# Expert rows of a mixture-of-experts layer: row fetches on two alternating semaphores, each issued ahead of the same turn's scatter

## The chip, the cores and the metric

One core of one Trainium2 chip. The metric is device time in microseconds (us) of one launch. Engines are named as the profile names them: PE is TensorE (PEld its weight loads), DVE is VectorE, ACT is ScalarE, POOL is GpSimd, SP is SyncE. Each has a sequencer of its own (a "q" behind the name, as in POOLq) that takes waits, branches and issues.

## What is computed

A graph layer on 12,500 nodes of 256 features, then a top-2 mixture of 64 experts, a batch normalisation and a residual layer normalisation. The change touches the experts alone:

```python
x = gc + (feats @ W_res + b_res)                 # per node, 256 wide
vals, idx = top_k(x @ Wg + bg, 2)                # two experts for each node
gates = softmax(vals)
# for every (node, expert) pair, by expert:
h1 = gelu(x[tok] @ w1[e] + b1[e])                # 256 -> 512
h2 = h1 @ w2[e] + b2[e]                          # 512 -> 256
core[tok] += gate * h2
```

## The kernel before

The program runs in stages: edges are sorted and counted, messages are gathered and summed (to about 2400 us), then `experts` (L1460) runs, then `norms`. In `experts` the pairs of one expert are cut into **turns** of 128 rows. The kernel works out at run time how many turns there are. 232 scatters were issued in the profiled execution, four of them after the last turn that has matmuls.

One turn g passes through the engines like this:

- **POOL** fetches the 128 rows of x of a turn with an indirect DMA (`fetch`, L1563 to L1566) into one of four places of `ring`, and later writes the turn's result rows out with another indirect DMA, a scatter into `picked` (`send`, L1568 to L1575). Row numbers are in `rows_at`, target rows in `places`.
- **ACT** copies the fetched rows to `xs` (`take`, L1537 to L1543) and applies the four gelus of the turn (L1548), in the order gelus of g, then `take(g + 2)`. After the last turn of an expert it also issues three DMAs that load the weights of an expert three ahead (`load_weights`, L275 to L277). The weights have four places.
- **PE** does sixteen matmuls with w1 (L1681), turns the next rows (two transposes, L1674), and does eight matmuls with w2 (L1688).
- **DVE** copies the turned rows (`xst`, L1621), adds b2 (`ysum`, L1648) and, in `scale` (L1625 to L1640), sets the next row numbers, the target rows and the gate, and multiplies into one of the **two** result buffers `ys[:, 0]` and `ys[:, 1]`.

What sets the order on POOL is the loop `quad` (L1586 to L1595), four turns a round. Step n of it is: wait until scatter n-1 has landed (`y_sent`, L1590), tell DVE that this buffer is free (`freed`, L1591), wait for DVE's result n (`y_set`, L1570), issue scatter n (L1573), wait until the fetches of all rows up to n+3 have landed (`rows_in`, L1593), issue the fetch of row block n+4. DVE's `scale(n)` waits for `freed` n+1 before it writes `places` (L1633), so scatter n-2 has landed by then. ACT's `take(g)` waits for `rows_in` itself. All fetches count up one semaphore, one after the other, and so never two are in flight.

Of the kernel before, what the change touches and what calls it, by code (L numbers as in the profile page):

```python
# [41 lines left out]
def gnn_layer(nc, x, src, dst, W_gc, b_gc, W_res, b_res, Wg, bg, w1, b1, w2, b2, gamma, beta, out):  # L42
# [35 lines left out]
    with ExitStack() as ctx:  # L78
# [178 lines left out]
        with ExitStack() as stage:  # L257
            def tmp(name, shape, dt):
                return stage.enter_context(nc.sbuf_tensor(name, shape, dt))

            HOT_W = 4 * (PER + 1) // 2 * P
            W1, W2 = HELD * KD * H, HELD * KH * D
            work = tmp("work", [P, (RING + 1) * (D + 1) + HOT_W], F32)
            assert W1 + W2 + HELD * D <= (RING + 1) * (D + 1)
            w1s = work[:, 0:W1].rearrange("p (u k h) -> p u k h", u=HELD, k=KD)
            w2s = work[:, W1:W1 + W2].rearrange("p (u k d) -> p u k d", u=HELD, k=KH)
            b2s = work[:, W1 + W2:W1 + W2 + HELD * D].rearrange("p (u d) -> p u d", u=HELD)
            table = tmp("table", [P, 4, (X + HELD) * (CAP // P)], F32)
            base_of = tmp("base_of", [1, X + 1 + HELD], I32)
            b1_cols = tmp("b1_cols", [P, KH, X], F32)  # L270
            w_in = [ctx.enter_context(nc.semaphore(f"w_in{u}")) for u in range(HELD)]

            def load_weights(eng, e, u):

                eng.dma_start(w1s[:, u, :, :], w1[bass.ds(e, 1), :, :].rearrange("a (k p) h -> p (a k) h", p=P)).then_inc(w_in[u], 16)  # L275
                eng.dma_start(w2s[:, u, :, :], w2[bass.ds(e, 1), :, :].rearrange("a (k p) d -> p (a k) d", p=P)).then_inc(w_in[u], 16)
                eng.dma_start(b2s[:, u, :], b2[bass.ds(e, 1), :].broadcast_to([P, D])).then_inc(w_in[u], 16)  # L277

            with nc.cleanup_on_exit():
                aggregate(nc, x, W_res, b_gc, b_res, W_gc, Wg, bg, b1, h_table, x1_rows, m_base, base_out, zeros_out, acc3, work, ident, ones,  # L280
                          iota_f, place_lo, src_cols, rel_cols, where, valid, table, base_of, b1_cols, load_weights, ps,
                          N=N, D=D, X=X, H=H, KD=KD, KH=KH, AW=AW, CH=CH, PER=PER, EARLY=EARLY, LATE=LATE, NT=NT, LAST=LAST)
            experts(nc, x1_rows, picked, w1s, w2s, b2s, w_in, load_weights, ident, table, base_of, b1_cols, ps, D=D, X=X, H=H, KD=KD, KH=KH,
                    ROW=ROW, PLACES=N * TOP_K)
# [1175 lines left out]
def experts(nc, x1_rows, picked, w1s, w2s, b2s, w_in, load_weights, ident, table, base_of, b1_cols, ps, D, X, H, KD, KH, ROW, PLACES):  # L1460

    with ExitStack() as part:
        def t2(name, shape, dt):
            return part.enter_context(nc.sbuf_tensor(name, shape, dt))

        def sem2(name):
            return nc.alloc_semaphore(name)

        U = HELD
        R = 4  # L1470
# [3 lines left out]
        rows_at = t2("rows_at", [P, R], I32)  # L1474
# [8 lines left out]
        ys = t2("ys", [P, 2, D], F32)  # L1483
        warm = t2("warm", [P, 1], F32)

        rows_in = sem2("ring_in")
        first_rows_at = sem2("first_rows_at")
        order_set = sem2("order_set")
        xs_set = sem2("xs_set")
# [8 lines left out]
        y_set = sem2("y_set")  # L1498
        y_sent = [sem2("y_sent0"), sem2("y_sent1")]
        freed = sem2("ys_freed")  # L1500
        carrier = sem2("x_carrier")

        def bounds(engine, e, more=0):

            _, g = nc.values_load_multi_w_load_instructions(
                base_of[0:1, bass.ds(e, U + 1 + more)], engines=[engine], min_val=0, max_val=X * CAP // SUP,
                skip_runtime_bounds_check_because="sums of the experts' turns, 1 to CAP // SUP each")
            return g

        def turns_in_all(engine):  # L1510
            return nc.values_load(base_of[0:1, X:X + 1], engines=[engine], min_val=X, max_val=X * CAP // SUP,
                                  skip_runtime_bounds_check_because="the sum of the experts' turns")

        def each_expert(eng, engine, before, turn, follow=None, more=0):


            def some(i, followed):
                starts = bounds(engine, U * i, more)
                for u in range(U):
                    e = U * i + u  # L1520
                    before(e, i, u, starts)
                    with eng.Fori(starts[u], starts[u + 1]) as g:
                        turn(e, u, g, starts[u])
                    if u < followed:
                        follow(e + U - 1, (u - 1) % U, starts[u])
            if follow is None:
                with eng.Fori(0, X // U) as i:
                    some(i, 0)
            else:
                with eng.Fori(0, X // U - 1) as i:  # L1530
                    some(i, U)
                some(X // U - 1, 1)

        with nc.Block() as block:
            @block.scalar
            def _(act):
                def take(g):  # L1537

                    act.wait_ge(rows_in, 16 * (g + 1))

                    if not isinstance(g, int) or g > 0:
                        act.wait_ge(xs_turned, g)
                    nc.scalar.copy(xs[:, :], ring[:, g % R, 0:D]).then_inc(xs_set, 1)  # L1543

                def turn(e, u, g, g0):
                    for h in range(KH):
                        act.wait_ge(h_done, g * KH + h + 1)
                        nc.scalar.activation(hid[:, h, :], ps[:, h, 0:SUP], ACT.Gelu,  # L1548
                                             bias=b1_cols[:, h, bass.ds(e, 1)]).then_inc(h_set, 1)
                    take(g + 2)  # L1550

                def follow(e, u, g0):

                    act.wait_ge(ysum_set, g0 + 1)
                    load_weights(act, e, u)

                nc.scalar.activation(warm[:, :], b1_cols[:, 0, 0:1], ACT.Gelu)
                take(0)
                take(1)
                each_expert(act, EngineType.Activation, lambda *a: None, turn, follow)  # L1560

            @block.gpsimd
            def _(pool):  # L1563
                def fetch(u):
                    pool.indirect_dma_start(out=ring[:, u, :], out_offset=None, in_=x1_rows[:, :],  # L1565
                                            in_offset=bass.IndirectOffsetOnAxis(ap=rows_at[:, u:u + 1], axis=0)).then_inc(rows_in, 16)  # L1566

                def send(n, u):  # L1568
                    b = u % 2
                    pool.wait_ge(y_set, n + 2)  # L1570
                    pool.sem_inc(carrier, 1)

                    pool.indirect_dma_start(out=picked[:, :], out_offset=bass.IndirectOffsetOnAxis(ap=places[:, b:b + 1], axis=0),  # L1573
                                            in_=ys[:, b, :], in_offset=None, bounds_check=PLACES - 1,
                                            oob_is_err=False).then_inc(y_sent[b], 16)  # L1575

                pool.wait_ge(first_rows_at, 1)
                for u in range(R):
                    if u > 0:
                        pool.wait_ge(rows_in, 16 * u)  # L1580
                    fetch(u)
                pool.sem_inc(freed, 1)

                quads = (turns_in_all(EngineType.Pool) + R) // R

                def quad(j):  # L1586
                    for u in range(R):
                        n = R * j + u
                        if not isinstance(n, int) or n > 0:
                            pool.wait_ge(y_sent[1 - u % 2], 32 * j + 16 * ((u + 1) // 2))  # L1590
                        pool.sem_inc(freed, 1)  # L1591
                        send(n, u)
                        pool.wait_ge(rows_in, 16 * (n + R))  # L1593
                        pool.sem_inc(carrier, 1)
                        fetch(u)  # L1595
                quad(0)
                with pool.Fori(1, quads) as j:
                    quad(j)
                pool.wait_ge(y_sent[0], 32 * quads)
                pool.sem_inc(carrier, 1)  # L1600
                pool.wait_ge(y_sent[1], 32 * quads)
                pool.sem_inc(carrier, 1)
                pool.wait_ge(rows_in, 64 * quads + 64)
                pool.sem_inc(carrier, 1)

            @block.vector
            def _(dve):
# [363 lines left out]
```

## Time and profile before

| what | us |
|---|---|
| median of 3 runs | 3764.92 (3763.87 to 3767.51) |
| the profiled execution | 3769.93 |
| its span in the profile | 3768.2 |
| first to last scatter of `experts` | 1019.3 (2429.6 to 3448.9) |
| PE busy in that stretch | 892.32, granted clock 0.99 |
| POOL busy in that stretch | 459.66 |
| one fetch, one scatter on POOL | 0.978, 1.011 |

A span is what the profiler saw between first and last instruction; 1.7 us lie around it. Busy time on POOL is the time in which it writes out a DMA's descriptors, not the transfer. The profiled execution is 5.0 us above the median. "Granted clock" is the share of TensorE's full clock that the chip let through, 1.00 for 2.4 GHz and 0.50 for 1.2 GHz.

### The profile page before, as it was taken

The numbers are of one execution on the slowest core, as the hardware profiler recorded it, in microseconds if no ns is written. First come the engines' busy times: TensorE is split into PE (matmuls) and PEld (weight loads), VectorE is DVE, ScalarE is ACT, GpSimd is POOL, SyncE is SP. The second block draws the span as 40 slices with busy tenths as digits, with TensorE's granted clock in tenths as the row PEclk, the third lists the DMA queues.
The fourth block names the chain that finished last, engine by engine and source line by source line (L and its number), as shares of the span: only waits on it lengthen the run. The fifth ranks groups of instructions, "written<-read, shape, count | busy, mean of one in ns | idle before, by whom it ended". The sixth has DMA issues, their size and how long they took to land. (4 is left out here: it accounts for less than half of the span.)

```text
span 3768.2 us, 61533 instructions
## 1 busy us (share of the span) xinstructions
PE 3028.5 (80%) x16520; PEld 2198.4 (58%) x16684; DVE 1867.6 (50%) x6028; ACT 1083.0 (29%) x2679; POOL 2136.5 (57%) x2194
## 2 busy tenths in 40 slices
PE   3747889898899888898998898789888898894710
PEld 3523555555555555555555555588777887884610
DVE  6982444444444444444444444544443444443878
ACT  3950222222222222222222222233333333331123
POOL 3006777777777777777777777244444444442122
PEclk9878999999999999999999999899999999997865
DMA  8635444444444444444444444334344343434634
GB/s 351 223 102 159 126 118 128 128 118 128 128 117 128 118 128 128 117 129 127 118 128 121 125 117 118 112 120 133 120 134 147 118 131 124 136 121 135 204 107 145
DMA packets 287579, 509.98 MB, mean 135 GB/s; under 512 B 43417, under 2 KB 201200, under 8 KB 284738
## 3 DMA queue, kind: packets, MB, share of 16 engines
q0 software_dynamic: 102192, 274.64, 25.7%
q10 hardware_dynamic: 73042, 123.41, 9.4%
q1 hardware_dynamic: 112192, 109.95, 9.1%
q8 instruction: 89, 1.46, 0.2%
q14 instruction: 64, 0.52, 0.0%
HBM read 404.99 MB, written 107.63 MB: 136 GB/s over the span
## 5 line engine op out<-in xcount | busy, mean ns | idle before, releaser
L1150 POOL DMA_INDIRECT work<-h_table,src_cols x1661 | 1575.5, 949 | 728.0 <-issue 426.2
L1436 PE MATMUL ps<-work 128*128 128x257 f32 x3322 | 1063.2, 402 | 208.5 <-DMA work<-h_table,src_cols 185.2
L1436 PEld LDWEIGHTS ps<-work 128*128 128x128 f32 x3322 | 563.8, 192 | 556.5 <-issue 301.5
L1342 PE MATMUL ps<-none_w,none 128*128 128x512 bf16 x2213 | 677.1, 383 | 5.5 <-issue 0.4
L1565 POOL DMA_INDIRECT ring<-x_rows,rows_at x236 | 230.8, 978 | 484.8 <-DMA ring<-x_rows,rows_at 235.5
L1688 PE MATMUL ps<-work,hid 128*128 128x256 f32 x1824 | 445.0, 387 | 72.5 <-ACT hid L1548 70.5
L1681 PEld LDWEIGHTS ps<-xst,work 128*128 128x128 f32 x3648 | 444.9, 193 | 25.6 <-issue 13.4
L1681 PE MATMUL ps<-xst,work 128*128 128x128 f32 x3648 | 448.6, 276 | 8.2 <-issue 7.4
L1185 DVE TENSOR_TENSOR acc<-acc,ps 128x257 f32<-128x257 f32 x98 | 41.5, 423 | 780.6 <-PE ps L1333 780.6
L1688 PEld LDWEIGHTS ps<-work,hid 128*128 128x128 f32 x1824 | 328.7, 190 | 134.3 <-ACT hid L1548 97.9
L1342 PEld LDWEIGHTS ps<-none_w,none 128*128 128x128 bf16 x2344 | 224.7, 99 | 160.1 <-issue 3.8
L1548 ACT ACTIVATE hid<-ps,b_cols 128x128 f32<-128x128 f32 x912 | 269.2, 368 | 142.8 <-PE ps L1681 99.2
L1573 POOL DMA_INDIRECT picked<-ys,places x232 | 234.6, 1011 | 127.6 <-issue 100.9
L1648 DVE TENSOR_TENSOR ysum<-ps,work 128x256 f32<-128x256 f32 x228 | 96.9, 425 | 397.9 <-PE ps L1688 397.9
L1170 DVE TENSOR_TENSOR work<-rel_cols,ps 128x1152 f32<-128x1152 f32 x196 | 250.6, 1280 | 64.2 <-PE ps L1436 63.4
L1543 ACT COPY xs<-ring 128x256 f32 (+1 forms) x230 | 93.1, 405 | 509.6 <-DMA ring<-x_rows,rows_at 509.6
L1116 ACT COPY acc<-ps 128x256 f32<-128x256 f32 x98 | 36.6, 373 | 651.0 <-PE ps L1375 651.0
L1122 ACT COPY turned<-ps 128x512 f32<-128x512 f32 x98 | 57.4, 586 | 473.3 <-PE ps L1362 473.3
L733 ACT ACTIVATE stairs<-iota_f,lo_half 128x128 bf16<-128x128 f32 x624 | 183.0, 388 | 32.9 <-DVE lo_half L675 32.0
L1795 POOL TENSOR_TENSOR pk<-pk,beta_b 128x1792 f32<-128x1792 f32 x14 | 64.1, 4585 | 225.2 <-DMA pk<-in_x_dram 225.2
L1205 DVE TENSOR_TENSOR logits<-ps,gate_bias 128x64 f32<-128x64 f32 x98 | 22.0, 225 | 281.3 <-PE ps L1389 281.3
L1621 DVE COPY xst<-ps 128x256 f32<-128x256 f32 x229 | 97.3, 425 | 121.9 <-PE ps L1674 112.4
(256 smaller groups left out, 3806.4 us busy)
## 6 DMA issues: line engine op xcount, KB each, us to landing
work<-in_L_gnn_w_dram ACTq DMA_DIRECT2D x122, 512.0 KB, 4.6
work<-h_table,src_cols POOLq DMA_INDIRECT x1661, 2.8
picked<-acc ACTq DMA_DIRECT2D x1, 25088.0 KB, 102.1
pk<-picked SPq DMA_DIRECT2D x28, 896.0 KB, 8.1
m_base<-acc ACTq DMA_DIRECT2D x1, 12642.0 KB, 37.0
acc<-m_base SPq DMA_DIRECT2D x14, 903.0 KB, 6.5
x_rows<-acc SPq DMA_DIRECT2D x98, 129.0 KB, 2.4
xr_x<-in_x_dram SPq DMA_DIRECT2D x97, 128.0 KB, 2.3
```

Source lines behind the costliest of these rows:

```text
L733: mm = nc.scalar.activation(stairs[:, k, n, :], iota_f[:, :], ACT.Sign, scale=-1.0, bias=lo_half[:, bass.ds(g * PIECES + 2 * WHOLE + n, 1)])
L1150: pool.indirect_dma_start(out=got[:, c % RING, 0:D], out_offset=None, in_=h_table[:, :], in_offset=bass.IndirectOffsetOnAxis(ap=src_cols[: ...
L1170: nc.vector.tensor_tensor(hot[:, (2 * t + h) % HOTS, 0:b - a, :], rel_cols[:, a:b].unsqueeze(2).broadcast_to([P, b - a, P]), lanes.unsquee ...
L1342: nc.tensor.matmul(ps[:, 7, :], none[:, :], none_w[:, :], start=False, stop=False)
L1436: nc.tensor.matmul(ps_flat[:, bank(t, k, w[0])], hot[:, (2 * t + (k >= HALF)) % HOTS, k % HALF if k >= HALF else k, :], got[:, c % RING, : ...
L1548: nc.scalar.activation(hid[:, h, :], ps[:, h, 0:SUP], ACT.Gelu, bias=b1_cols[:, h, bass.ds(e, 1)]).then_inc(h_set, 1)
L1565: pool.indirect_dma_start(out=ring[:, u, :], out_offset=None, in_=x1_rows[:, :], in_offset=bass.IndirectOffsetOnAxis(ap=rows_at[:, u:u + 1 ...
L1573: pool.indirect_dma_start(out=picked[:, :], out_offset=bass.IndirectOffsetOnAxis(ap=places[:, b:b + 1], axis=0), in_=ys[:, b, :], in_offse ...
L1621: nc.vector.tensor_copy(xst[:, :, :], ps[:, 6, 0:KD * SUP].rearrange("p (k n) -> p k n", k=KD)).then_inc(xst_set, 1)
L1648: nc.vector.tensor_tensor(ysum[:, :], ps[:, 4, 0:D], b2s[:, u, :], ALU.add).then_inc(ysum_set, 1)
L1681: mm = nc.tensor.matmul(ps[:, h, 0:SUP], w1s[:, u, k, h * P:(h + 1) * P], xst[:, k, :], start=(k == 0), stop=(k == KD - 1))
L1688: mm = nc.tensor.matmul(ps[:, 4, 0:D], hid[:, h, :], w2s[:, u, h, :], start=(h == 0), stop=(h == KH - 1))
```

## The change

The fetches use two semaphores by turns (even and odd row blocks), so that two fetches may be in flight. ACT no longer waits for a fetch itself but for `rows_ready`, which POOL counts up once it has seen a fetch land. In a step, POOL now waits for row block n+2 (instead of n+3), counts up `rows_ready`, waits for scatter n-1 and for result n as before, and then issues the fetch of block n+4 and behind it scatter n. The result buffers stay two.

```diff
-        rows_in = sem2("ring_in")
+        rows_in = [sem2("ring_in0"), sem2("ring_in1")]
+        rows_ready = sem2("rows_ready")
...
                 def take(g):
-                    act.wait_ge(rows_in, 16 * (g + 1))
+                    act.wait_ge(rows_ready, g + 1)
...
-                                            in_offset=bass.IndirectOffsetOnAxis(ap=rows_at[:, u:u + 1], axis=0)).then_inc(rows_in, 16)
+                                            in_offset=bass.IndirectOffsetOnAxis(ap=rows_at[:, u:u + 1], axis=0)).then_inc(rows_in[u % 2], 16)
...
                 def send(n, u):
                     b = u % 2
-                    pool.wait_ge(y_set, n + 2)
-                    pool.sem_inc(carrier, 1)
...
-                for u in range(R):
-                    if u > 0:
-                        pool.wait_ge(rows_in, 16 * u)
-                    fetch(u)
+                fetch(0)
+                fetch(1)
+                for u in range(2):
+                    pool.wait_ge(rows_in[u], 16)
+                    pool.sem_inc(rows_ready, 1)
+                    fetch(u + 2)
...
                         n = R * j + u
+                        pool.wait_ge(rows_in[u % 2], 32 * j + 16 * (u // 2 + 2))
+                        pool.sem_inc(rows_ready, 1)
                         if not isinstance(n, int) or n > 0:
                             pool.wait_ge(y_sent[1 - u % 2], 32 * j + 16 * ((u + 1) // 2))
                         pool.sem_inc(freed, 1)
-                        send(n, u)
-                        pool.wait_ge(rows_in, 16 * (n + R))
+                        pool.wait_ge(y_set, n + 2)
                         pool.sem_inc(carrier, 1)
                         fetch(u)
+                        send(n, u)
```

On POOL, in the first two steps of the loop (before the counted rounds begin). The list names semaphores by the number's first owner: before, `x_in_any` is the fetches' `rows_in`, `any_gathered3` is `y_set`, `any_gathered4` and `any_gathered5` are `y_sent` 0 and 1. Before:

```order
L1573 DMA picked<-ys,places 25088x256 [waits any_gathered3]
L1565 DMA ring<-x_rows,rows_at 128x258 [waits x_in_any]
L1573 DMA picked<-ys,places 25088x256 [waits any_gathered4,any_gathered3]
L1565 DMA ring<-x_rows,rows_at 128x258 [waits x_in_any]
L1573 DMA picked<-ys,places 25088x256 [waits any_gathered5,any_gathered3]
```

After the change `x_in_any` and `scaled_any` are the two semaphores of the fetches, `any_gathered5` is `y_set`, `any_gathered6` and `any_gathered7` are `y_sent` 0 and 1:

```order
L1565 DMA ring<-x_rows,rows_at 128x258 [waits x_in_any,any_gathered5]
L1570 DMA picked<-ys,places 25088x256
L1565 DMA ring<-x_rows,rows_at 128x258 [waits scaled_any,any_gathered6,any_gathered5]
L1570 DMA picked<-ys,places 25088x256
L1565 DMA ring<-x_rows,rows_at 128x258 [waits x_in_any,any_gathered7,any_gathered5]
```

All waits of a step now stand ahead of its fetch, the one for the scatter before (`y_sent`) among them, and the scatter comes last, with no wait of its own.

## Rows read from the trace of the kernel before

**Rows 1.** Whole page: its head and costliest groups (count, busy, mean ns, idle before).

```profile
span 3768.2 us, 61533 instructions
...
L1565 POOL DMA_INDIRECT ring<-x_rows,rows_at x236 | 230.8, 978 | 484.8 <-DMA ring<-x_rows,rows_at 235.5
...
L1573 POOL DMA_INDIRECT picked<-ys,places x232 | 234.6, 1011 | 127.6 <-issue 100.9
```

**Rows 2.** Windows from first to last scatter: busy (count) by engine, clock, DMA share.

```profile
2429.60:3448.90 1019.30, 892.32 (x5881) 802.69 (x5879) 430.81 (x1671) 357.13 (x1130) 459.66 (x462) 0.99 0.40 126
```

**Rows 3.** Waits, 2650 to 3450 us: total us, times, longest.

```profile
ACT xs L1543 <- DMA ring<-x_rows,rows_at: 403.1, 177, 4.5
...
POOL ring L1565 <- DMA ring<-x_rows,rows_at: 182.1, 120, 4.1
POOL ring L1565 <- DMA picked<-ys,places: 148.0, 47, 4.3
```

**Rows 4.** Timeline, 3006 to 3020 us: start, duration, engine, line, idle before and releaser.

```profile
3006.84 0.98 POOL L1565 DMA_INDIRECT ring<-x_rows,rows_at  x1 [1.99 <-DVE ys L1639]
3008.13 1.01 POOL L1573 DMA_INDIRECT picked<-ys,places  x1 [0.30 <-issue]
...
3008.97 1.95 PE L1681 MATMUL ps<-xst,work 128*128 128x128 f32 x16
...
3010.41 0.98 POOL L1565 DMA_INDIRECT ring<-x_rows,rows_at  x1 [1.27 <-DMA ring<-x_rows,rows_at]
...
3012.70 1.95 PE L1681 MATMUL ps<-xst,work 128*128 128x128 f32 x16
...
3013.40 0.41 ACT L1543 COPY xs<-ring 128x256 f32 x1 [1.97 <-DMA ring<-x_rows,rows_at]
...
3013.75 0.38 ACTq L275 DMA_DIRECT2D work<-in_L_gnn_w_dram  x1
...
3013.95 0.98 POOL L1565 DMA_INDIRECT ring<-x_rows,rows_at  x1 [1.21 <-DMA ring<-x_rows,rows_at]
...
3019.93 0.98 POOL L1565 DMA_INDIRECT ring<-x_rows,rows_at  x1 [3.45 <-DMA picked<-ys,places]
```

**Rows 5.** All instructions of line L275 (weight loads) issued by ACT.

```profile
L275 ACTq DMA_DIRECT2D work<-in_L_gnn_w_dram x61: 383/385/434, 2434.3 to 3393.5; - x61
```

**Rows 6.** Timeline, 3403 to 3411 us, POOL.

```profile
3403.70 1.01 POOL L1573 DMA_INDIRECT picked<-ys,places  x1 [2.89 <-issue]
...
3407.22 1.10 POOL L1573 DMA_INDIRECT picked<-ys,places  x1 [1.23 <-issue]
...
3410.77 1.01 POOL L1573 DMA_INDIRECT picked<-ys,places  x1 [1.16 <-DMA picked<-ys,places]
```

**Rows 7.** Timeline, 3433 to 3440 us, behind the last matmuls.

```profile
3433.84 0.98 POOL L1565 DMA_INDIRECT ring<-x_rows,rows_at  x1 [2.41 <-DMA ring<-x_rows,rows_at]
3434.23 0.15 DVE L1633 CAST places<-in_order  x1 [2.39 <-POOLq L1591]
...
3435.13 1.01 POOL L1573 DMA_INDIRECT picked<-ys,places  x1 [0.30 <-issue]
...
3439.85 1.01 POOL L1573 DMA_INDIRECT picked<-ys,places  x1 [0.30 <-DVE ys L1639]
```

**Rows 8.** Timeline, 2433 to 2438 us: scatters around a weight load.

```profile
2433.53 1.00 POOL L1573 DMA_INDIRECT picked<-ys,places  x1 [1.65 <-issue]
...
2434.30 0.43 ACTq L275 DMA_DIRECT2D work<-in_L_gnn_w_dram  x1
...
2437.04 1.00 POOL L1573 DMA_INDIRECT picked<-ys,places  x1 [1.23 <-issue]
```

**Rows 9.** Timeline, 3161 to 3169 us: a scatter right behind a weight load.

```profile
3161.57 0.38 ACTq L275 DMA_DIRECT2D work<-in_L_gnn_w_dram  x1
...
3162.27 1.02 POOL L1573 DMA_INDIRECT picked<-ys,places  x1 [3.12 <-issue]
...
3168.16 0.15 DVE L1633 CAST places<-in_order  x1 [1.57 <-POOLq L1591]
```

**Rows 10.** Timeline (two rows) and windows (the third) around 2460 us.

```profile
2461.46 2.40 PE L1688 MATMUL ps<-work,hid 128*128 128x256 f32 x8 [2.93 <-ACT hid L1548]
...
2463.66 3.22 PE L1681 MATMUL ps<-xst,work 128*128 128x128 f32 x16
...
2463.00:2466.00 3.00, 3.00 (x14) 2.83 (x13) 1.41 (x6) 1.07 (x3) 0.98 (x1) 0.50 0.04 12
```

More of the change, by code:

```diff
@@ L1602, in _ @@
                 pool.sem_inc(carrier, 1)
-                pool.wait_ge(rows_in, 64 * quads + 64)
-                pool.sem_inc(carrier, 1)
+                for u in range(2):
+                    pool.wait_ge(rows_in[u], 32 * quads + 32)
+                    pool.sem_inc(carrier, 1)
             @block.vector
```

## Prediction

> **What bounds the kernel now.** I read the page first, then the windows, the waits and the timeline of `experts`. The reader should see on the page that POOL issues 236 fetches and 232 scatters of about 1 us each [rows 1]. In the windows, the stretch from first to last scatter is 1019.3 us, so a turn costs 1019.3 / 232 = 4.39 us; PE is busy for 892.32 of it, and its clock is full [rows 2]. In the waits, ACT waits 177 times for a fetch, 403.1 us in 800, and POOL waits again and again for a landing before its next fetch [rows 3].
>
> The timeline says why. Two chains run nearly at the same pace. Undisturbed, PE starts a turn's w1 matmuls 3.73 us after the last turn's (3008.97 to 3012.70), and the fetches, one at a time, start 3.54 to 3.57 us apart (3006.84, 3010.41, 3013.95) [rows 4]. Then ACT issues a weight load (L275 at 3013.75), the fetch issued 0.20 us behind it is held up, and the next fetch starts only 5.98 us later, at 3019.93: 2.42 us more than 3.56 [rows 4]. The row names the scatter as releaser, but the code waits there for the fetch alone. There are 61 such loads [rows 5], and between them the fetches catch up 0.17 us a turn at best. As a sum: 232 x 3.73 + 61 x 2.42 = 865 + 148 = 1013, against 1019.3 measured. So the bound is PE's turn, plus a fetch that is held up once for each expert. The change aims at the second term.
>
> **The change part by part.**
>
> *Fetches.* With two in flight and the fetch ahead of the scatter, a fetch issued in step n is wanted in step n+2, two periods later. Even a held one, landed within the 5.98 us to the next fetch's start, comes in time. This takes the 148 us away, if nothing else binds.
>
> *The scatter's landing.* The wait for scatter n-1 stood ahead of scatter n before as well, but the fetch did not stand behind it: POOL wrote the fetch's descriptors while the scatter was in flight. Now step n is: scatter n-1 lands, then the fetch of block n+4 (0.98 us), then scatter n. Everything is in series on one engine, and with two result buffers and this wait there is one scatter in flight. What the scatter chain costs alone is seen where no fetch lies between: 3403.70, 3407.22, 3410.77, which is 3.52 and 3.55 us [rows 6], the last with the scatter's landing as its releaser; another pair gives 3.51 [rows 8]. The fetch adds its 0.98 and the 0.30 that lie between a fetch and the scatter behind it [rows 4]. That makes 3.53 + 1.28 = 4.81 us a turn. It is the upper bound: part of the 3.53 is the start of a scatter behind its wait, and a fetch may start a little faster (0.2 less is my lower bound, 4.6). Near the end of the stage, where no matmul is left, the old kernel runs a similar pattern, fetch, 0.30, scatter, and its scatters stand 4.72 us apart (3435.13, 3439.85) [rows 7]; another wait binds there, but dispatch and landings are alike. I take **4.72**.
>
> This is above PE's 3.73, so POOL sets the pace: 232 x 4.72 = 1095.0 us. Who waits: DVE at `places` for `freed`, ACT at `take` for `rows_ready`, and so PE, about 0.9 us in each turn. ACT's `take(g+2)`, its gelus and PE's w2 behind it fit into a period (0.41 + 3.73 is below 4.72), so they hide. At 4.72 us a step and some 3 us of landing, two fetches are hardly ever in flight together.
>
> *The weight loads.* They still come 61 times [rows 5]. Now the transfer on the path is the scatter, so what matters is where a scatter stands to a load. A scatter 0.77 us ahead of the load went through free (2433.53 against 2434.30, next scatter 3.51 later) [rows 8]. A fetch 0.20 behind was held [rows 4], and a scatter 0.70 behind was held too: DVE learnt of its landing only at 3168.16, 5.89 us after its start at 3162.27 [rows 9]. Where will it stand after? ACT issues a load 0.35 us behind a `take` (3013.40, 3013.75) [rows 4], and `take` is now released by POOL's sequencer once it has handed on the scatter. That sequencer runs ahead of its engine: at 3434.23 DVE had been released by L1591, which stands behind the fetch in the program, while that fetch still ran (3433.84 to 3434.82) [rows 7]. If it is ahead by the length of the fetch or so, `rows_ready` comes 0.8 us ahead of the scatter's start, `take` 0.2 later, the load 0.35 later: the scatter starts about 0.25 us behind the load and is held. If it only comes when the scatter starts, the scatter is 0.5 ahead of the load, between the free case and the held one. I take held, since one case of running ahead is on record. Its price: at least the fetch's 2.42; at most 5.89 less an ordinary landing of about 2.5 (3.53 less about 1 for the start), 3.4. I take **2.8** for each, nearer the fetch, as no held fetch stands ahead of it any more: 61 x 2.8 = 171 us.
>
> *Small things.* The first row blocks come up to 3 us sooner, beside weights that PE still loads: nothing. The count-ups of `rows_ready` ride on waits. PE's idle of about 0.9 + 2.8 us in a held period may lower its clock: after a gap of 2.93 us the clock was 0.50 and sixteen matmuls took 3.22 instead of 1.95 us [rows 10, 4]. That costs PE 1.3 to 3 us (3.22 less 1.95, and as much again for w2), where it has 0.9 spare each turn; and its result has a lead: `take(g+2)` falls ahead of scatter g-1, w2 and DVE then need about 1.9 + 1.5 us, and POOL wants result g only behind the landing of scatter g-1 or later. So nothing in the sum, and up to 1 us x 61 in the bound above.
>
> *Sum.* 1095.0 + 171 = 1266, less 1019.3: **+246.5 us**. From the profiled execution, 3769.9 + 246.5 = 4016.4; it lies 5.0 above the median, so the median to come is **4011**.
>
> **The rivals.**
>
> *A. The scatter's landing does not bind (faster).* If POOL could start the next fetch without feeling the landing, PE would be the bound and the held fetches hidden: 1019.3 less about 148 + 6, so about 3611; each load also keeps ACT from its gelus, 2.93 us of PE's time in one case [rows 10], and with 1 us as my estimate of the mean, 61 us: 3611 to 3672. For it: the waits for fetches are the largest in the list. Against it: the wait for scatter n-1 is in every step, and the order of the program puts the fetch behind it. The Trainium skill (DMA: Bandwidth & Descriptors, Rules for kernel authors) says to issue a DMA early and wait on its semaphore late, so that the fixed cost overlaps; for the fetch the change does so, for the scatter it undoes it. By the rule read for the fetch alone this rival would win. Chance 0.05.
>
> *B. As forecast, but loads miss the scatter.* `rows_ready` comes late enough that the scatter is out before the load's packets flow: +75.7 us at 4.72, 3841 (3813 at 4.6). Chance 0.18.
>
> *C. The clock falls for good.* PE idles in each turn; at 1.2 GHz a turn takes twice 3.73 = 7.46 us, above POOL's period: 232 x 7.46 = 1731, 4476. The decision lies with the gaps: one of 2.93 us was followed by a low stretch [rows 10], but the whole stage with its 1 us gaps had a mean of 0.99 [rows 2]. The Trainium skill (TensorE: Matmul & The Clock Gate, HAM oscillation) tells of a kernel that went cold anew in every tile because of its DMA waits; by that, each held turn would begin cold and then recover, which costs the sum nothing as long as PE's slack holds. Chance 0.03 for the full fall.
>
> *D. As forecast with dearer holds.* 4.81 and 3.4 plus up to 1 us of clock: 1116 + 207 + 61 = 1384, +365, 4130. Chance 0.08 for the part above 4085.
>
> **How the numbers follow.** The forecast has 0.66: 4.6 to 4.81 a turn and 2.42 to 3.4 for each hold give 1067 + 148 = 1215 to 1116 + 207 = 1323, 3961 to 4069. The range reaches down to B at 4.72 and a little into D: 3835 to 4085. Some 0.2 lies outside it (A, half of B's lower part, C, D). A measurement of this kernel can tell about 0.2% (7.5 us) from no change. Faster 0.06 (A and a little for what I don't see), same 0.02, slower 0.92.
>
> **What would show it.** In the trace after: scatters 4.7 us apart in ordinary turns and the fetch 1.28 us ahead of each; POOL's idle time before the fetch put down to the scatter's landing (`picked`), hardly to `ring`; one period of about 7.5 us for each weight load, with L275 issued 0.2 to 0.3 us ahead of a scatter; ACT's wait before `xs` put down to POOLq; DVE waiting at `places`; PE busy near 0.7 of the stage. Wrong would be: periods near 3.7 (A), no long periods (B), or a granted clock below 0.9 (C).

## The result: 4031.6 us, 7% slower

The changed kernel takes **4031.61 us** (median, 4028.55 to 4031.91), the old one 3765.05 us beside it: ratio **1.0705** (95% interval 1.0687 to 1.0724). The forecast was 4011, range 3835 to 4085. One execution of e8 below took 7756.35 us, over twice its other three, and is left out of its ratio.

The page of the changed kernel: head, the costliest groups that answer to [rows 1], and the clock's row of the slices.

```profile
span 4026.8 us, 61423 instructions
...
PEclk8869999999999999999999999999999999997865
...
L1565 POOL DMA_INDIRECT ring<-x_rows,rows_at x236 | 233.8, 991 | 796.8 <-DMA picked<-ys,places 745.6
...
L1543 ACT COPY xs<-ring 128x256 f32 (+1 forms) x230 | 93.0, 404 | 772.6 <-POOLq L1589 768.1
L1570 POOL DMA_INDIRECT picked<-ys,places x232 | 235.0, 1013 | 80.1 <-issue 80.1
```

POOL's work is the same, 0.99 and 1.01 us a DMA. What changed is the idle time before the fetch: 484.8 us before, 796.8 now, and 745.6 of it ends with the landing of a scatter. The window from first to last scatter, called the stage here, as [rows 2] (its length, busy time and count of PE, PEld, DVE, ACT and POOL, then the granted clock, DMA share and GB/s):

```profile
2429.10:3716.00 1286.90, 997.70 (x5862) 856.65 (x5860) 431.90 (x1666) 354.85 (x1131) 463.06 (x462) 0.93 0.33 99
```

1286.9 us against 1019.3: all of the loss lies here. The timeline of one load, the place that answers to [rows 4] (POOL, ACT's `xs` and L275, and DVE's `places`, which is L1635 now):

```profile
3183.77 1.01 POOL L1570 DMA_INDIRECT picked<-ys,places  x1 [0.30 <-issue]
...
3187.17 0.97 POOL L1565 DMA_INDIRECT ring<-x_rows,rows_at  x1 [2.39 <-DMA picked<-ys,places]
...
3187.80 0.41 ACT L1543 COPY xs<-ring 128x256 f32 x1 [2.74 <-POOLq L1589]
...
3188.15 0.38 ACTq L275 DMA_DIRECT2D work<-in_L_gnn_w_dram  x1
...
3188.45 1.01 POOL L1570 DMA_INDIRECT picked<-ys,places  x1 [0.31 <-issue]
...
3194.33 0.15 DVE L1635 CAST places<-in_order  x1 [1.14 <-POOLq L1592]
...
3195.03 1.06 POOL L1565 DMA_INDIRECT ring<-x_rows,rows_at  x1 [5.56 <-DMA picked<-ys,places]
...
3196.39 1.01 POOL L1570 DMA_INDIRECT picked<-ys,places  x1 [0.30 <-issue]
...
3200.73 1.01 POOL L1570 DMA_INDIRECT picked<-ys,places  x1 [0.30 <-issue]
```

An ordinary step is 4.68 us from scatter to scatter (3183.77, 3188.45): landing, 0.97 of fetch, 0.30, scatter. The scatter that starts 0.30 us behind the load (3188.15) is held, and the next one starts only 7.94 later. Of the 231 distances between scatters in the whole timeline, the 61 that begin at the scatter nearest to a load have a mean of 8.05 us, the other 170 one of 4.68. In 49 of the 61 that scatter starts 0.14 to 0.45 us behind the load, in 12 it starts 0.07 ahead of it, and those are held too. A **hold** is what such a distance has more than an ordinary step. All scatters together, by their line:

```profile
L1570 POOL DMA_INDIRECT picked<-ys,places x232: 997/1012/1117, 2429.1 to 3716.0; - x116
...
DMA to landing us min/median/max: 2.1/2.5/8.1
```

### The profile page after: what moved, and what is told of

Its sections match the earlier page's. It is cut to its first block and busy times, and to the rows that moved or that the text cites. A ratio compares the mean times of both kernels' runs of the same rounds, so it can differ in the third digit from the quotient of the medians.

```text
span 4026.8 us, 61423 instructions
## 1 busy us (share of the span) xinstructions
PE 3133.3 (78%) x16520; PEld 2247.2 (56%) x16684; DVE 1867.3 (46%) x6028; ACT 1080.2 (27%) x2679; POOL 2137.9 (53%) x2194
## 5 line engine op out<-in xcount | busy, mean ns | idle before, releaser
L1565 POOL DMA_INDIRECT ring<-x_rows,rows_at x236 | 233.8, 991 | 796.8 <-DMA picked<-ys,places 745.6
L1690 PE MATMUL ps<-work,hid 128*128 128x256 f32 x1824 | 504.5, 425 | 109.2 <-ACT hid L1548 104.9
L1683 PEld LDWEIGHTS ps<-xst,work 128*128 128x128 f32 x3648 | 463.9, 199 | 30.8 <-issue 14.7
L1683 PE MATMUL ps<-xst,work 128*128 128x128 f32 x3648 | 463.4, 282 | 9.1 <-issue 8.4
L1690 PEld LDWEIGHTS ps<-work,hid 128*128 128x128 f32 x1824 | 359.4, 207 | 196.8 <-ACT hid L1548 148.9
L1543 ACT COPY xs<-ring 128x256 f32 (+1 forms) x230 | 93.0, 404 | 772.6 <-POOLq L1589 768.1
L1676 PE MATMUL ps<-ident,xs 128*128 128x128 f32 x458 | 98.9, 298 | 154.3 <-ACT xs L1543 152.4
```

The source lines that it names most:

```text
L1676: mm = nc.tensor.transpose(ps[:, 6, k * SUP:(k + 1) * SUP], xs[:, k * P:(k + 1) * P], ident[:, :])
L1683: mm = nc.tensor.matmul(ps[:, h, 0:SUP], w1s[:, u, k, h * P:(h + 1) * P], xst[:, k, :], start=(k == 0), stop=(k == KD - 1))
L1690: mm = nc.tensor.matmul(ps[:, 4, 0:D], hid[:, h, :], w2s[:, u, h, :], start=(h == 0), stop=(h == KH - 1))
```

## The experiments

Theory **S**: the fetch stands in series behind the scatter's landing (4.68 us a step), and each load holds a scatter. Rival **R**: what costs is that ACT hears of a landed fetch only through POOL. All kernels of the experiments have the masks of e1's note; the old and the changed kernel do not. Where the old kernel's time is given beside a run, it is that of the same series.

### e1: the order put back, the rest of the change kept

```diff
                         pool.wait_ge(y_set, n + 2)
                         pool.sem_inc(carrier, 1)
-                        fetch(u)
                         send(n, u)
+                        fetch(u)
```

> The changed kernel with one thing put back: in each step the scatter is issued ahead of the fetch. Two fetch semaphores, rows_ready and two result buffers stay. (In this and all following kernels the loaded turn counts are masked to ten bits, one register operation each, with no effect on the values.) Theory S (the fetch stands in series behind the scatter's landing, 4.68 us a step, and held scatters cost 3.4 us 61 times): a step falls back to the scatter's own 3.5 us, below PE's 3.73, so 232 x 3.73 plus holds of 2.4 to 3.4 x 61, 1013 to 1072 us of stage against 1019 before: 3760 to 3820 us, most likely 3780. Rival R (what costs is that ACT hears of a landing only through POOL): ACT's wait stays as late as in the changed kernel, so above 3900.

Measured: 3698.74 us beside 3774.74, ratio to before 0.9811 (0.9771 to 0.9851), 1.9% **faster than the old kernel** (the interval does not settle whether it is 2%). R is out: `rows_ready` is in it. S had the direction and missed the size, 3780 being 80 too much. The window, and the timeline around a load:

```profile
2433.10:3379.90 946.80, 880.48 (x5881) 799.60 (x5879) 432.74 (x1671) 385.82 (x1131) 459.50 (x462) 0.99 0.44 135
```

```profile
2995.09 1.01 POOL L1570 DMA_INDIRECT picked<-ys,places  x1 [1.28 <-DVE ys L1641]
...
2996.31 0.38 ACTq L275 DMA_DIRECT2D work<-in_L_gnn_w_dram  x1
2996.41 0.98 POOL L1565 DMA_INDIRECT ring<-x_rows,rows_at  x1 [0.30 <-issue]
2998.82 1.01 POOL L1570 DMA_INDIRECT picked<-ys,places  x1 [1.44 <-DVE ys L1641]
3000.14 0.98 POOL L1565 DMA_INDIRECT ring<-x_rows,rows_at  x1 [0.30 <-issue]
3003.64 1.01 POOL L1570 DMA_INDIRECT picked<-ys,places  x1 [2.53 <-issue]
```

The scatter is 1.22 us ahead of the load and goes free: the next starts 3.73 later, at PE's pace. The fetch issued 0.10 behind the load does not stop POOL, which issues another at 3000.14. The scatter at 2998.82, 2.51 behind the load, is held: of the 25 scatters of e1 that stand 2.2 to 2.8 us behind a load and whose landing the trace tells, the median lands 3.80 us after its start, where 2.45 is ordinary. So the scatter after it comes late (3003.64, 4.82 after). The half of the change that the diff names first, two fetch semaphores and `rows_ready`, is worth 1019.3 - 946.8 = 72.5 us of stage. The other half, the order, takes it away and costs 1286.9 - 946.8 = 340 us.

### e2: the order alone, on the old kernel

```diff
-                        send(n, u)
+                        pool.wait_ge(y_set, n + 2)
+                        pool.sem_inc(carrier, 1)
                         pool.wait_ge(rows_in, 16 * (n + R))
                         pool.sem_inc(carrier, 1)
                         fetch(u)
+                        send(n, u)
```

(with the wait for `y_set` taken out of `send`)

> The old kernel with the order of the change alone: one fetch semaphore, ACT waits for the fetches itself, two result buffers, but the fetch of a step is issued ahead of its scatter, behind all of the step's waits. Theory S: the same series of landing, fetch and scatter, so scatters 4.7 us apart and about the changed kernel's time, 4010 to 4050. Rival R: without rows_ready it is as fast as before, 3765.

Measured: 3945.64 us beside 3774.74, ratio 1.0466 (1.0410 to 1.0521), a **miss** for the size: R's 3765 is far off, and S has the mechanism, but even the lower end of its forecast is 64 too high. The stage:

```profile
2433.30:3630.10 1196.80, 972.35 (x5875) 840.83 (x5873) 430.29 (x1671) 359.72 (x1130) 460.01 (x463) 0.95 0.34 107
```

The order alone costs 1196.8 - 1019.3 = 177.5 us. Ordinary steps take 4.79 (median), a little more than in the changed kernel. The holds are what is smaller:

```profile
2986.79 0.38 ACTq L275 DMA_DIRECT2D work<-in_L_gnn_w_dram  x1
...
2989.39 1.01 POOL L1570 DMA_INDIRECT picked<-ys,places  x1 [0.30 <-issue]
...
2995.21 1.01 POOL L1570 DMA_INDIRECT picked<-ys,places  x1 [0.31 <-issue]
```

ACT waits for the fetch itself here, so its load falls elsewhere in the step. The next scatter stands 2.60 us behind the load, and its period is 5.82, not 7.94. In the changed kernel the load stands 0.3 us ahead of a scatter. The sum would account for the remaining 90 us (1286.9 - 1196.8): about 61 x 2, less 232 x 0.11. It is a sum and not an experiment: the two kernels also differ in the second fetch semaphore.

### e3: four result buffers, the change kept

```diff
-        places = t2("places", [P, 2], I32)
+        places = t2("places", [P, 4], I32)
...
-        ys = t2("ys", [P, 2, D], F32)
+        ys = t2("ys", [P, 4, D], F32)
...
-        y_sent = [sem2("y_sent0"), sem2("y_sent1")]
+        y_sent = [sem2(f"y_sent{b}") for b in range(4)]
...
-                    b = n % 2
+                    b = n % 4
...
-                            pool.wait_ge(y_sent[1 - u % 2], 32 * j + 16 * ((u + 1) // 2))
+                            pool.wait_ge(y_sent[(u + 1) % 4], 16 * j + 16 * (u // 3))
```

> The changed kernel with four result buffers (ys, places and y_sent by four), so that a step waits for scatter n-3 instead of n-1. Theory S: no landing is in series any more, held scatters and fetches are hidden, PE's 3.73 is the bound with about 1 us for each of 61 weight loads while ACT issues them: 865 + 61 = 926 us of stage, 3672 (3611 to 3710). Rival W (the wait for the scatter is cheap, and what costs is POOL's work order, descriptors of the fetch ahead of the result): no better than 3765 and more likely near 4030, since the order stays.

Measured: 3642.69 us (3630.89 to 3657.75) beside 3774.74, ratio 0.9655 (0.9602 to 0.9709). The order on POOL is that of the change, so rival W is out: what the order costs in the change, it costs through the wait for the last scatter. The window, and the first of the waits (2650 to 3300 us):

```profile
2429.80:3336.10 906.30, 863.82 (x5860) 795.50 (x5860) 417.47 (x1665) 398.34 (x1131) 458.49 (x463) 0.99 0.46 141
```

```profile
POOL ring L1565 <- DVE ys L1640: 268.0, 162, 5.0
```

POOL now waits for DVE's result, no longer for a landing. PE is busy for 863.8 of 906.3 us. The stage is 20 below the 926 forecast: what is left above PE's 865 is 0.7 us a load instead of 1.

### e4, e5: no weight loads

Both leave out 60 of the 61 loads, so later experts compute with the weights of the first four and the results are not the layer's. They serve for the timing alone.

```diff
                     act.wait_ge(ysum_set, g0 + 1)
-                    load_weights(act, e, u)
...
-                    pe.wait_ge(w_in[u], 48 * (i + 1))
+                    pe.wait_ge(w_in[u], 48)
```

> The changed kernel without the weight loads inside the experts' stage but the first four experts' (60 fewer; later experts use the first four's weights). Theory S: each load holds one scatter for 8.05 - 4.68 = 3.37 us, so the time falls by 60 x 3.37 = 202 to 3829, all steps near 4.68. If the loads only cost what they cost before (2.42 each) it falls by 145 to 3886; if they cost nothing, 4031.

Measured, on the changed kernel: 3837.16 us beside 3774.74, ratio 1.0178 (1.0124 to 1.0232), stage:

```profile
2434.50:3518.80 1084.30, 941.85 (x5860) 807.32 (x5860) 439.24 (x1665) 352.23 (x1131) 459.69 (x462) 0.99 0.18 52
```

(1286.9 - 1084.3) / 60 = **3.38 us a load**, as the periods said (8.05 - 4.68 = 3.37). The steps are 4.69 in the mean, so the series of landing, fetch and scatter is there with hardly a load. It also settles the clock: the mean rises from 0.93 to 0.99, yet the time falls by the holds alone. PE's stretches of low clock were covered by the waits.

> The old kernel without the weight loads inside the stage but the first four experts' (later experts use the first four's weights). Theory S: what a load costs the old kernel is one held fetch, 2.42 each, so 60 fewer give 145: 3765 - 145 = 3620, all turns near PE's 3.73. If ACT's time for the issue is what costs, the fall is smaller (60 x 1 = 60: 3705).

Measured, on the old kernel: 3638.95 us beside 3769.71, ratio 0.9656 (0.9637 to 0.9676), 19 above the forecast. The stage:

```profile
2434.40:3320.90 886.50, 851.66 (x5881) 796.51 (x5879) 435.06 (x1671) 414.14 (x1130) 459.31 (x463) 0.99 0.22 63
```

(1019.3 - 886.5) / 60 = 2.2 us a load, in which the hold and ACT's time for the issue are not parted. A load cost the old kernel 2.2 and costs the changed one 3.4.

### e6: four result buffers on the old kernel

> The old kernel (one fetch semaphore, scatter ahead of the fetch, ACT waits for fetches itself) with four result buffers. Theory S: the old kernel is bound by PE and the single fetch in flight, held once for each load; the scatter's landing does not bind, so 3750 to 3775, no gain. If the landing of the scatter already cost the old kernel something, 3700 or below.

Measured: 3756.53 us (3752.36 to 3761.6) beside 3769.71, ratio 0.9966 (0.9955 to 0.9977), stage 1004.9. As forecast: the scatter's landing hardly bound the old kernel, and buffers alone bring 13 us. They are worth 1286.9 - 906.3 = 381 us of stage in the changed one.

### e7, e10, e11: where the load falls

```diff
-                        pool.wait_ge(rows_in[u % 2], 32 * j + 16 * (u // 2 + 2))
-                        pool.sem_inc(rows_ready, 1)
                         if not isinstance(n, int) or n > 0:
                             pool.wait_ge(y_sent[1 - u % 2], 32 * j + 16 * ((u + 1) // 2))
                         pool.sem_inc(freed, 1)
+                        pool.wait_ge(rows_in[u % 2], 32 * j + 16 * (u // 2 + 2))
+                        pool.sem_inc(rows_ready, 1)
```

> The changed kernel with one thing moved: POOL counts up rows_ready behind the wait for scatter n-1, not ahead of it. ACT's take, and with it the weight load, falls some 2.5 us later, when no scatter is in flight. Theory P (the size of a hold is set by where the scatter stands to the load): ordinary steps stay 4.7; the load now catches the fetch, and the next scatter stands some 1.8 us behind it and lands with it 6.1 us behind the load, a hold of about 1.9 instead of 3.4: 4031 - 61 x 1.5 = 3940. Rival R (ACT's late hearing costs): later still, so slower than 4031.

Measured: 4051.23 us beside 3769.71, a **miss**: 111 above the forecast. The stage is 1296.4 us, 9.5 longer than the change's, so the time came out as rival R said. The load does fall where it was meant to, with the next scatter 1.52 us behind it:

```profile
3007.58 0.38 ACTq L275 DMA_DIRECT2D work<-in_L_gnn_w_dram  x1
...
3009.10 1.01 POOL L1570 DMA_INDIRECT picked<-ys,places  x1 [0.30 <-issue]
...
3014.66 0.98 POOL L1565 DMA_INDIRECT ring<-x_rows,rows_at  x1 [4.55 <-issue]
3015.94 1.01 POOL L1570 DMA_INDIRECT picked<-ys,places  x1 [0.30 <-issue]
```

This period is 6.84, though the 61 have a mean of 7.63. The ordinary steps rose to 4.89 in the mean. The page shows why: most of POOL's idle time before the fetch is now put down to DVE's result.

```profile
L1565 POOL DMA_INDIRECT ring<-x_rows,rows_at x236 | 230.4, 976 | 810.2 <-DVE ys L1641 537.1
```

With `take` behind the landing, ACT, PE and DVE have less time for the result. That is R's mechanism, a later `rows_ready` that costs time; e1 shows no such cost where POOL counts up as early as in the change and the scatter goes first. So the edit moved two things, and cannot price the place alone. e10 comes nearer, where SP's sequencer issues the loads. ACT is then also free of the issue, so what e10 gains is the most that the place alone can be worth:

```diff
-                each_expert(act, EngineType.Activation, lambda *a: None, turn, follow)
+                each_expert(act, EngineType.Activation, lambda *a: None, turn)
+
+            @block.sync
+            def _(sp):
+                def loads(i, n):
+                    starts = bounds(EngineType.SP, U * i)
+                    for u in range(n):
+                        sp.wait_ge(ysum_set, starts[u] + 1)
+                        load_weights(sp, U * i + u + U - 1, (u - 1) % U)
+                with sp.Fori(0, X // U - 1) as i:
+                    loads(i, U)
+                loads(X // U - 1, 1)
```

> The changed kernel (two result buffers) with the weight loads issued by SP instead of ACT. Theory P (a hold is set by where the scatter stands to the load): the load falls about 3 us behind a scatter's start, so the next scatter stands 1.5 to 1.8 us behind the load and lands 6.1 behind it, a hold of 2.1 instead of 3.4, with ordinary steps at 4.68: 4031 - 61 x 1.3 = 3950 (3920 to 3980). Unlike in e7, nothing else is moved. If a hold does not depend on the place, 4031.

> The changed kernel with nothing but the masks on the loaded turn counts that all these kernels have. Both theories: 4031 within 8 us. A difference would be the price of the masks in all of them.

These two and e9 ran in a series in which the old kernel took 4146.36 us (4138.17 to 4152.74); the stages ahead of the experts were some 375 us longer there (e11's first fetch starts at 2789.1 us, the changed kernel's at 2413.4). The record puts this series on chip 9, e12 on chip 13 and e1 to e8 on chip 0. So the stage is compared. e11 is the changed kernel with the masks: 4401.06 us, ratio 1.0616 (1.0593 to 1.0639), stage 1276.4, where the change had 1286.9. Its "4031 within 8 us" could not be tested in absolute time; in the stage the masks cost nothing that shows. The 10.5 us between these two are taken below as what a stage can differ by from chip to chip. e11's stage, and then e10's (4369.5 us, ratio 1.0540, 1.0506 to 1.0573):

```profile
2805.40:4081.80 1276.40, 994.25 (x5862) 844.77 (x5860) 436.08 (x1666) 354.71 (x1131) 463.09 (x462) 0.94 0.33 100
```

```profile
2806.00:4047.10 1241.10, 997.42 (x5862) 852.29 (x5860) 436.72 (x1666) 362.04 (x1131) 464.37 (x463) 0.93 0.33 102
```

35 us less than e11, where 81 were forecast. So the place is worth less than said, even if all of it is put down to the place. One hold of e10, where the load's row reads SPq:

```profile
3339.21 0.38 SPq L275 DMA_DIRECT2D work<-in_L_gnn_w_dram  x1
...
3340.91 1.01 POOL L1581 DMA_INDIRECT picked<-ys,places  x1 [0.30 <-issue]
...
3347.75 1.01 POOL L1581 DMA_INDIRECT picked<-ys,places  x1 [0.30 <-issue]
```

Put side by side, by the medians over the loads (the held scatter is the first one issued behind the load):

| kernel | held scatter starts behind the load | it lands behind the load | next scatter starts behind the load |
|---|---|---|---|
| the change | 0.30 | 5.92 | 8.31 |
| e7 | 1.52 | 6.17 | 8.99 |
| e10 | 1.64 | not told | 8.60 |
| e2 | 2.58 | 6.30 | 8.66 |

A held scatter thus lands some 6 us behind the load's issue, wherever it started, and what the hold costs is that moment less what had passed already. The gain from a later place is not one for one: from e11 to e10 the scatter moved from 0.23 to 1.64 us behind the load, and its period fell from 7.83 to 7.10 (medians).

### e8, e12: does the order matter with four buffers?

> Four result buffers, two fetch semaphores and rows_ready, but the scatter ahead of the fetch. Theory S: with four buffers the order on POOL no longer matters, so within 15 us of the changed kernel with four buffers (3643), PE's turn being the bound in both. If the order still matters (POOL's engine time), more than 30 us apart.

Measured: 3687.52 us beside 3769.71, ratio 0.9785 (0.9766 to 0.9805), 45 us above e3's median: a **miss**, since at most 15 were forecast. The stage is 939.2 against e3's 906.3, 33 us more, so with four buffers the order still matters, and the other way round: here the fetch goes better first.

> As e8 (four result buffers, two fetch semaphores, scatter ahead of the fetch), but SP issues the weight loads. It asks why e8's stage was 33 us longer than e3's, 939 against 906, though only POOL's order differed. Theory H (in e8 the load was issued just ahead of a fetch, which was held, and POOL's next rows_ready waited for it; in e3 the load caught a scatter, which four buffers hide): with SP's load some 3 us ahead of a scatter in both orders, nothing that is wanted soon is held, so the first to last scatter is within 10 us of e9's 879. Rival O (scatter first is dearer by itself): about 33 above e9, 912.

Measured: 4002.68 us beside 4119.72 (ratio 0.9689, 0.9644 to 0.9734), stage 899.2, against e9's 879.1: 20 above, between H's 10 and O's 33. The two ran on different chips, and 10.5 us is what the change itself differs by between two chips, so neither is shown; what part of POOL's order costs in e8 stays open.

### e9: four buffers, loads issued by SP

> The changed kernel with four result buffers, and the weight loads issued by SP's sequencer (idle in this stage) instead of ACT's, as soon as DVE has the sum of an expert's last turn. Theory A (what is left above PE's 3.73 a turn is mostly ACT, which issues a load for 1.7 us while its gelus wait): the stage falls from 906 to about 865 + 15, so 3643 - 25 = 3618 (3605 to 3635). Rival: the load's transfers then hold something that is not hidden, or ACT's issue was never on the path: 3643 or more.

Measured: 4007.94 us beside 4146.36, ratio 0.9665 (0.9648 to 0.9682), 138 us less than the old kernel. Its stage, from an execution of 3975.49 us (the other four took 4003 to 4010; from the last scatter to the end it has 286.6 us where e12 has 318.1, so what it saved lies behind the experts):

```profile
2808.00:3687.10 879.10, 849.01 (x5862) 789.21 (x5860) 417.93 (x1666) 392.76 (x1131) 459.46 (x463) 0.99 0.46 144
```

27 less than e3, where 25 were forecast, and 14 above 232 x 3.73. It is the shortest stage of all runs, but e3 ran on another chip, so the size of the gain is uncertain by some 10 us. e3 and e9 leave nothing of the work out and beat both kernels. In whole time the two can't be ranked, since they ran in different series.

| kernel | fetch ahead | fetches in flight | result buffers | stage, us |
|---|---|---|---|---|
| before | no | 1 | 2 | 1019.3 |
| e6 | no | 1 | 4 | 1004.9 |
| e2 | yes | 1 | 2 | 1196.8 |
| after | yes | 2 | 2 | 1286.9 |
| e1 | no | 2 | 2 | 946.8 |
| e8 | no | 2 | 4 | 939.2 |
| e3 | yes | 2 | 4 | 906.3 |
| e12 (loads by SP, chip 13) | no | 2 | 4 | 899.2 |
| e9 (loads by SP, chip 9) | yes | 2 | 4 | 879.1 |

## Why the prediction was right

*What bounds before.* PE's 3.73 a turn and one held fetch a load: e5 took the loads away and the stage fell to 886.5, 21 above 865. Right, with 2.2 for a load (hold and issue together) where 2.42 was read for the hold.

*The ordinary step.* 4.72 forecast, 4.68 measured, with the series that was named: the wait before the fetch is put down to the scatter (745.6 us of 796.8), the fetch runs 1.28 us ahead of its scatter. The upper bound of 4.81 was not reached. 231 x 4.68 = 1081 against 1095 in the sum. One thing in the list of who waits was wrong: DVE was to wait at `places` in each turn, and waited there 42 times in all, 54.4 us. What slowed PE was ACT's wait before `take`, 768.1 us.

*The loads.* The choice between held and free scatters was the weak point (0.66 against 0.18), and the place was met: L275 stands 0.30 us ahead of the scatter in the median, 0.25 was forecast. The choice of "held" rested on one row; it did not hang on those tenths, since the 12 scatters that start 0.07 us ahead of the load are held as well. POOL's sequencer does run ahead of its engine, as the one row [rows 7] let suppose: `take` starts at 3187.80, while the fetch ahead of the scatter still runs. The size was set too low: 2.8 taken, 3.37 measured, at the top end of 3.4. 61 x 0.57 = 35 us is more than the 20.6 that the forecast was short by. The 2.8 leaned on the held fetch; the scatter of [rows 9] was the nearer kin.

*The sum.* 1266 forecast, 1286.9 measured: -14 from the steps, +35 from the holds. That these two have opposite signs is luck. So is that two things outside the sum nearly cancel: from the last scatter to the end the kernel took 310.8 us instead of 319.3, and the profiled execution lay 3.1 below its median, where 5.0 above was carried over.

*The rivals.* A needed the landing not to bind; e3 shows what it would have looked like, 906 us. B is e4's picture, 1084 against the 1095 given. C did not come: 0.93 in the stage, with stretches like this one after a held scatter (a window of the changed kernel), which cost nothing by e4. They do show in PE's busy share, 997.70 of 1286.90 or 0.78, where 0.7 was named as a sign.

```profile
3022.40:3025.80 3.40, 3.40 (x13) 2.95 (x12) 1.00 (x5) 0.53 (x2) 1.06 (x2) 0.50 0.04 13
```

The Trainium skill (TensorE: Matmul & The Clock Gate, HAM oscillation) says that waits for DMAs between short bursts send the array cold again each time. The trace agrees in part: the clock was at its low level in 42 stretches, 175 us of the stage, for 61 holds, and all but the last, which reaches past the stage's end, ended within it.

*What I did not see.* The prediction gave the first half of the change 148 us "if nothing else binds", and nothing in the sum, since the landing binds. That was right for this kernel. What the half is worth alone, with the scatter first, was not worked out; e1 finds 72.5, and my 3780 for e1 counted full holds, though its scatter goes ahead of the load and only the next one is held, for less.

## What to carry to other kernels

When one engine issues a fetch and a store in turn, and a step waits for the last store's landing, put the store first: what stands between that landing and the next store is added to every step (e1 against the change, 340 us). Before raising the number of fetches in flight, look at the wait on the other side. Here the same two semaphores gave 72.5 us with the store first and two result buffers, none with the fetch first and two (e2 1196.8, the change 1286.9), and with the fetch first and four the stage fell to 906.3. Once no landing is in series, the order can be worth little and the other way round (e3 and e8, 33 us). A burst of bulk loads holds small transfers that are issued at its side or up to 2.6 us behind it, so look where in the step such a load is issued (e10 against e11, 35 us at most for the place).

## What the runs showed of the hardware

- A small indirect DMA issued within some 2.6 us behind a load of 1.1 MB (two of 512 KB and one of 128) lands about 6 us behind the load's issue: scatters in the median 5.92 (issued 0.30 behind), 6.17 (1.52) and 6.30 (2.58), where an ordinary one lands 2.45 us after its own start. The 12 that started 0.07 us ahead of the load were held too (5.2 us to landing); those issued 0.77 [rows 8] or 1.22 us ahead (e1) were free.
- A sequencer hands on two DMAs to GpSimd before the first is written out: ACT's `take`, which is released only behind both, starts 0.63 us behind the start of the fetch (3187.17, 3187.80) and 0.65 ahead of the scatter's.
- The same program's earlier stages were some 375 us longer in one series than in another, on another chip, while its experts' stage agreed within 1% (1276.4 and 1286.9). Whether the chip is the cause was not looked for.
